# One layer's mixture of experts: residual on GpSimd, one sum over eight on VectorE, early relus all on ScalarE, router scratch in PSUM

## What is computed

```python
x = x + 0.5 * _L0_ffn_ref(_layernorm(x), ...)    # 16 experts 128->256->128, gelu, top 2
x = x + _L0_attn_ref(_layernorm(x), ...)         # linear attention over a sequence, gelu
x = x + 0.5 * _L0_ffn_ref(_layernorm(x), ...)
x = x + 0.5 * _L1_ffn_ref(_layernorm(x), ...)    # 16 experts 128->128, relu, top 2
x = x + _L1_attn_ref(_layernorm(x), ...)         # causal linear attention, 16 heads of 8
x = x + 0.5 * _L1_ffn_ref(_layernorm(x), ...)
```

```python
y = jax.nn.relu(jnp.einsum('nh,edh->ned', flat, expert_w) + expert_b[None, :, :])
sel = jnp.take_along_axis(y, flat_idx[:, :, None], axis=1)
out = jnp.sum(sel * flat_w[:, :, None], axis=1)
```

## Time and profile before

| what | value |
|---|---|
| median of 3 runs | 738.96 us (737.16 to 744.51) |
| the profiled execution | 736.88 us, of which the span of the trace 735.2 us |
| PE busy | 656.1 us (89%) |
| DVE busy | 509.0 us (69%) |
| ACT busy | 403.9 us (55%) |
| POOL busy | 214.4 us (29%) |
| granted TensorE clock, mean | 0.955 |

### The profile page before, as it was taken

The page is one execution under the profiler, slowest core; times in us unless marked ns, Lnnn a source line. Parts: engine busy times, 40 slices in busy tenths (PEclk is TensorE's granted clock), DMA queues, the critical chain, the costliest instruction groups (busy, mean ns, idle before and its releaser), DMA issues.

```text
span 735.2 us, 7595 instructions
## 1 busy us (share of the span) xinstructions
PE 656.1 (89%) x2395; PEld 417.7 (57%) x2395; DVE 509.0 (69%) x1139; ACT 403.9 (55%) x795; POOL 214.4 (29%) x148
## 2 busy tenths in 40 slices
PE   3699998999999999999999998999999869868693
PEld 2456565555555565665666665566666445555472
DVE  5587457647446636658599687869776468688887
ACT  4254464546545544766754695584476325745394
POOL 2120010110002202181320364041037136775367
PEclk9899998999999999999999999999999969989897
DMA  8772522053243134512223232103221000000001
GB/s 244 153 152 63 111 58 58 20 97 58 60 105 66 59 68 79 73 26 46 58 58 70 48 58 58 57 3 91 72 41 27 1 0 0 1 0 16 14 1 29
DMA packets 27027, 42.23 MB, mean 57 GB/s; under 512 B 1689, under 2 KB 8938, under 8 KB 26986
## 3 DMA queue, kind: packets, MB, share of 16 engines
q1 hardware_dynamic: 26986, 41.74, 26.5%
HBM read 40.42 MB, written 1.31 MB: 57 GB/s over the span
## 4 chain that ended last, share of the span: by engine, by line
PE 38%; DVE 25%; issue 19%; POOL 11%; ACT 6%; DMA 0%; SPq 0%; DVEq 0%; POOLq 0%; ACTq 0%
PE py L1103 14%; PE ph L882 4%; PE ph L883 4%; PE ph L884 4%; POOL stage L440 3%; POOL rstd L387 3%; POOL stage L444 3%; DVE xn L659 2%; DVE red L769 2%; DVE hw L841 2%; ACT stage L528 2%; DVE stage L766 1%; DVE stage L736 1%; DVE X L771 1%; PE ps L1057 1%
## 5 line engine op out<-in xcount | busy, mean ns | idle before, releaser
L577 ACT ACTIVATE g<-ph,b1col 128x512 f32<-128x512 f32 x256 | 171.9, 689 | 146.6 <-PE ph L884 111.8
L1103 PE MATMUL py<-hw,w2s 128*128 128x512 f32 x512 | 249.0, 611 | 2.4 <-DVE hw L841 2.4
L841 DVE TENSOR_TENSOR hw<-g,bc 128x1024 f32<-128x1024 f32 x128 | 166.1, 1301 | 94.7 <-ACT g L577 93.2
L387 POOL TENSOR_TENSOR rstd<-vare,mhalf 128x4 f32<-128x4 f32 x24 | 36.6, 1524 | 392.2 <-DVE vare L653 392.2
L1103 PEld LDWEIGHTS py<-hw,w2s 128*128 128x128 f32 x512 | 97.6, 194 | 78.5 <-issue 64.9
L882 PE MATMUL ph<-xbh,w1h 128*128 128x512 f32 x256 | 135.1, 528 | 0.0
L528 ACT ACTIVATE stage<-ps,comb 128x128 f32<-128x128 f32 x288 | 84.1, 514 | 44.4 <-PE ps L1013 28.5
L883 PE MATMUL ph<-xbl,w1h 128*128 128x512 f32 x256 | 103.4, 404 | 0.0
L884 PE MATMUL ph<-xbh,w1l 128*128 128x512 f32 x256 | 103.3, 404 | 0.0
L882 PEld LDWEIGHTS ph<-xbh,w1h 128*128 128x128 f32 x256 | 49.9, 195 | 28.5 <-issue 20.6
L883 PEld LDWEIGHTS ph<-xbl,w1h 128*128 128x128 f32 x256 | 50.1, 196 | 24.0 <-issue 17.0
(11 more groups left out here) (207 smaller groups left out, 959.7 us busy)
## 6 DMA issues: line engine op xcount, KB each, us to landing
bc<-comb_rows SPq DMA_DIRECT2D x31, 1024.0 KB, 8.5
stage<-in_L_ffn_W_dram SPq DMA_DIRECT2D x4, 512.0 KB, 6.9
X<-in_L_attn_x_dram SPq DMA_DIRECT2D x4, 256.0 KB, 3.3
bc<-comb_rows SPq DMA_DIRECT2D x4, 256.0 KB, 5.6
out_dram<-X SPq DMA_DIRECT2D x4, 256.0 KB, 2.3
comb_rows<-combT SPq DMA_DIRECT2D x8, 32.0 KB, 2.1
side<-in_L_attn_wq_dram SPq DMA_DIRECT2D x1, 64.0 KB
side<-in_L_attn_wk_dram SPq DMA_DIRECT2D x1, 64.0 KB
```

Of the source, the lines that this page charges most:

```text
L387: nc.gpsimd.tensor_tensor(rstd[:, 0:n], vare[:, 0:n], mhalf[:, 0:n], ALU.pow).then_inc(light["rstd"], 1)
L577: nc.scalar.activation(g[:, s % 2, h, 0:w], ph[:, (HC * s + h) % RING_PH, 0:w], ACT.Gelu, bias=b1col[:, HC * e + h:HC * e + h + 1]).then_i ...
L841: V.tensor_tensor(hw[:, s % RING_HW, :, 0:w], g[:, s % 2, :, 0:w], bc[:, s // GQ % 2, s % GQ, 0:w].unsqueeze(1).to_broadcast([P, HC, w]), ...
L1103: ins = T.matmul(py[:, 0:cols], w2s[:, w], hw[:, s2 % RING_HW, h, 0:cols], start=e2 == 0 and h == 0, stop=False)
```

## The change

- `ACT_GROUPS` becomes (4, 3): for early tiles ACT makes all four groups (16 instructions a tile), and DVE's L756 goes; late tiles stay at 3 and 1.
- POOL adds the two halves of an early tile in one instruction over 1024 numbers. For late tiles it keeps two of 512. The third addition (L444, L766) goes for all tiles.
- DVE sums over eight in one instruction over 1024 numbers, into one of two buffers.
- The residual goes from DVE to POOL, an addition of 128 numbers a tile, one step behind in POOL's program. The factor 0.5 goes into `comb`. ACT's wait for a free buffer is now for the sum (`sum`), not for the residual; `red` is still the residual.
- In the router `lgs`, `oh1`, `selm`, `topf`, `s_all` and `s_rec` lie in the unused half of the PSUM bank `pl`. A light stage after `rt` waits for `comb` in place of `shift`.
- `LIGHT` starts with the chunks 0, 1, 2 in place of 0, 2, 1, and ATT0's second norm comes one place later. `TURNS` is written anew.

```diff
-    ACT_GROUPS = 3
+    ACT_GROUPS = (4, 3)
+    QUARTERED = {(MOE1_A, 0): False, (MOE1_B, 0): False, (MOE1_A, 1): False, (MOE1_B, 1): False}
...
+        small = pl[:, CH // 2:CH]
+        lgs, oh1, selm = (small[:, i * TPC * E:(i + 1) * TPC * E].rearrange("p (t e) -> p t e", t=TPC) for i in range(3))
...
             def f1_(l, c):
...
+                def residual(j):
+                    pool.wait_ge(signal["sum"], n + j + 1)
+                    nc.gpsimd.tensor_tensor(X[:, tile_(c, j)], X[:, tile_(c, j)], total[:, (n + j) % 2, :], ALU.add).then_inc(signal["red"], 1)
...
-                    pool.wait_ge(signal["relu_a"], (n + j + 1) * ACT_GROUPS)
-                    nc.gpsimd.tensor_tensor(r0, r0, r1, ALU.add).then_inc(signal["half"], 1)
+                    if acts == GROUPS:
+                        pool.wait_ge(signal["relu_a"], (n + j + 1) * acts)
+                        both, other = (r[:, j % 2, a * E * D // 2:(a + 1) * E * D // 2] for a in range(2))
+                        nc.gpsimd.tensor_tensor(both, both, other, ALU.add).then_inc(signal["half"], 2)
...
                     yield
+                    if j:
+                        residual(j - 1)
+                        yield
+                residual(ntiles(c) - 1)
+                yield
...
-                                act.wait_ge(signal["red"], n + j - 1)
+                                act.wait_ge(signal["sum"], n + j - 1)
...
-                V.tensor_tensor(comb[:, tiles(c), :], t_(pm), r_(s_rec).unsqueeze(2).to_broadcast([P, n, E]), ALU.mult).then_inc(light["comb"], 1)
+                V.scalar_tensor_tensor(comb[:, tiles(c), :], t_(pm), 1.0 if moe0(l) else 0.5, r_(s_rec).unsqueeze(2).to_broadcast([P, n, E]),
+                                       ALU.mult, ALU.mult).then_inc(light["comb"], 1)
...
-                        r0, r2 = (r[:, j % 2, a * E * D // 4:(a + 1) * E * D // 4] for a in (0, 2))
-                        (klink if late else hlink)(V.tensor_tensor(r0, r0, r2, ALU.add))
-                    if j:
-                        dve.wait_ge(signal["red"], n + j)
-                    (klink if late else hlink)(V.tensor_reduce(sum_[:, :], r[:, j % 2, 0:E * D // 4].rearrange("p (d e) -> p d e", d=D), AX, ALU.add))
-                    xs_ = X[:, tile_(c, j)]
-                    ins = V.scalar_tensor_tensor(xs_, sum_[:, :], 0.5, xs_, ALU.mult, ALU.add)
-                    ins.then_inc(signal["red"], 1)
+                        V.tensor_reduce(sums, r[:, j % 2, 0:E * D // 2].rearrange("p (a d e) -> p d a e", a=2, d=D), mybir.AxisListType.XY, ALU.add).then_inc(signal["sum"], 1)
...
-                    signal = {"ln": "xl", "rt": "shift", "ct": "ct"}[last]
+                    signal = {"ln": "xl", "rt": "comb", "ct": "ct"}[last]
```

More of the change, by code:

```diff
@@ L114, in build_program @@
         topi = sb("topi", [P, TPC, 8], mybir.dt.uint32)
[L115 to L118, removed]
+        shf, exs = (sb(n, [P, TPC, E]) for n in ("shf", "exs"))
+        oh2, pm = (sb(n, [P, TPC, E]) for n in ("oh2", "pm"))
+        s_top, s_den = (sb(n, [P, TPC]) for n in ("s_top", "s_den"))
         comb = sb("comb", [P, TILES, E])
@@ L156, in build_program @@
         ps = ctx.enter_context(nc.psum_tensor("ps", [P, 3, CH], f32))
+        small = pl[:, CH // 2:CH]
+        lgs, oh1, selm = (small[:, i * TPC * E:(i + 1) * TPC * E].rearrange("p (t e) -> p t e", t=TPC) for i in range(3))
+        topf = small[:, 3 * TPC * E:3 * TPC * E + 2 * TPC].rearrange("p (t a) -> p t a", t=TPC)
+        s_all, s_rec = (small[:, 3 * TPC * E + i * TPC:3 * TPC * E + (i + 1) * TPC] for i in (2, 3))
         def by_tile(buffer, i):
@@ L203, in build_program @@
                                           "vz", "o_ps", "o", "x")}
-        f1 = {(l, late): {n: sem(f"f{l}_{late}_{n}") for n in ("y_ps", "relu_a", "relu_v", "half", "quarter", "red")}
+        f1 = {(l, late): {n: sem(f"f{l}_{late}_{n}") for n in ("y_ps", "relu_a", "relu_v", "half", "quarter", "sum", "red")}
               for l in (MOE1_A, MOE1_B) for late in (0, 1)}
@@ L434, in f1_ @@
                 r = rel_late if late else rel
+                acts = ACT_GROUPS[late]
+                total = red_late if late else red
+                def residual(j):
+                    pool.wait_ge(signal["sum"], n + j + 1)
+                    nc.gpsimd.tensor_tensor(X[:, tile_(c, j)], X[:, tile_(c, j)], total[:, (n + j) % 2, :], ALU.add).then_inc(signal["red"], 1)
                 for j in range(ntiles(c)):
-                    pool.wait_ge(signal["relu_a"], (n + j + 1) * ACT_GROUPS)
@@ L442, in f1_ @@
-                    if l == MOE1_A:
+                    if acts == GROUPS:
+                        pool.wait_ge(signal["relu_a"], (n + j + 1) * acts)
+                        both, other = (r[:, j % 2, a * E * D // 2:(a + 1) * E * D // 2] for a in range(2))
+                        nc.gpsimd.tensor_tensor(both, both, other, ALU.add).then_inc(signal["half"], 2)
+                    else:
+                        pool.wait_ge(signal["relu_a"], (n + j + 1) * acts)
+                        nc.gpsimd.tensor_tensor(r0, r0, r2, ALU.add).then_inc(signal["half"], 1)
+                        pool.wait_ge(signal["relu_v"], (n + j + 1) * (GROUPS - acts))
+                        nc.gpsimd.tensor_tensor(r1.rearrange("p (d e) -> p d e", d=D), r1.rearrange("p (d e) -> p d e", d=D),
+                                                r3.rearrange("p (e d) -> p d e", d=D), ALU.add).then_inc(signal["half"], 1)
@@ L443, in f1_ @@
+                    if QUARTERED[l, late]:
                         pool.wait_ge(signal["half"], 2 * (n + j + 1))
-                        nc.gpsimd.tensor_tensor(r0, r0, r2, ALU.add).then_inc(signal["quarter"], 1)
+                        nc.gpsimd.tensor_tensor(r0, r0, r1, ALU.add).then_inc(signal["quarter"], 1)
                     yield
+                    if j:
[3 more added lines that the diff above has]
+                yield
@@ L520, in f1_ @@
                     for q in range(GROUPS):
-                        if q < ACT_GROUPS:
+                        if q < acts:
                             u = (n + j) * GROUPS + q
@@ L747, in f1_ @@
                 late, signal, n = moe1(l, c)
-                banks, r, sum_ = (ph, rel_late, red_late) if late else (ps, rel, red)
+                banks, r, total = (ph, rel_late, red_late) if late else (ps, rel, red)
+                acts = ACT_GROUPS[late]
                 for j in range(ntiles(c)):
                     for q in range(GROUPS):
-                        if q >= ACT_GROUPS:
+                        if q >= acts:
                             if j == 0:
@@ L760, in f1_ @@
                         yield
-                    if l == MOE1_A:
+                    if n + j >= 2:
+                        dve.wait_ge(signal["red"], n + j - 1)
+                    sums = total[:, (n + j) % 2, :]
+                    if QUARTERED[l, late]:
                         dve.wait_ge(signal["quarter"], n + j + 1)
+                        V.tensor_reduce(sums, r[:, j % 2, 0:E * D // 4].rearrange("p (d e) -> p d e", d=D), AX, ALU.add).then_inc(signal["sum"], 1)
                     else:
                         dve.wait_ge(signal["half"], 2 * (n + j + 1))
-                        r0, r2 = (r[:, j % 2, a * E * D // 4:(a + 1) * E * D // 4] for a in (0, 2))
-                        (klink if late else hlink)(V.tensor_tensor(r0, r0, r2, ALU.add))
-                    if j:
-                        dve.wait_ge(signal["red"], n + j)
-                    (klink if late else hlink)(V.tensor_reduce(sum_[:, :], r[:, j % 2, 0:E * D // 4].rearrange("p (d e) -> p d e", d=D), AX, ALU.add))
-                    xs_ = X[:, tile_(c, j)]
-                    ins = V.scalar_tensor_tensor(xs_, sum_[:, :], 0.5, xs_, ALU.mult, ALU.add)
-                    ins.then_inc(signal["red"], 1)
+                        V.tensor_reduce(sums, r[:, j % 2, 0:E * D // 2].rearrange("p (a d e) -> p d a e", a=2, d=D), mybir.AxisListType.XY, ALU.add).then_inc(signal["sum"], 1)
                     yield
```

19 lines of the change are left out of this document (8 added, 11 removed), and 37 rows, old and new, of the table TURNS.

## The result

The changed kernel takes 715.52 us (median of 4 runs, 707.71 to 716.92), the kernel before 741.49 us in the same session (4 runs). The ratio is 0.963, with a 95% interval of 0.954 to 0.972: 20 to 34 us faster. I had forecast 730.5 with a range from 721 to 744, so the sign was right and the time lies outside the range. The profiled execution took 716.92 us, its span is 714.9 us: 20.3 less than before. The medians lie 26.0 us apart. The profile of before is of an execution faster than any of its four timed ones, that of after is of the slowest of four, so the profiles say where 20.3 us went and nothing of the rest. Ratios are of fast runs only; an execution 1.5% or more above the fastest of its kernel counts as slow, and as e5's profile is of such a one, no marks are read from it.

What follows compares the result with a forecast made beforehand. PE was taken to bound the main stream, a chain across engines the tail. Main part +1.5 and tail -10.0 gave -8.5 us, from the median 738.96 to 730.5, with a range of 721 to 744.

Steps and rivals of the forecast that it cites:

- That part is bound by PE: Main stream, 40 to 575 us: PE busy 513 of 535 us, so PE bounds it; main part forecast at +1.5 us.
- ACT's relus in the main part: Main part: 13.4 us of relus added on ACT, mostly hidden; +2.5 us in all, ends -1 and +13.
- rival 2: MOE1 stretches of the main stream: ACT's relu bursts delay gelus and PE stands; slower, 747.4 us, chance 0.13.
- The router: Sixteen router passes with six results in PSUM, and the wait for `comb` in place of `shift`: 0 us.
- 642 to 650 us: Tail, ATT1's last norm: ACT with its 64 relus takes the place of DVE, 0 us.
- 655.9 to 662.8 us: Tail: the epilogue on POOL and DVE ends before attention needs POOL, PE's wait goes; -4.5 us, ends 1.7 and 6.8.
- 668 to 691 us: Tail chain: two sums of 1.22 replace additions, sums, residual and relu near 5.1 us; -2.6 us, ends 0 and 5.
- the last norm and router: Tail, 691 to 706 us: addition, sum and residual ahead of `xn` go, router pairs lighter; -2.0 us, ends 0 and 2.6.
- Behind the last `comb`: End of the kernel, after 705.8 us: ACT's 76 relus set the pace, 25.7 for 26.6 us; -0.9, ends 0 and 2.
- The tail: From 575 to 735 us, a chain going from engine to engine; its four terms were to save 10.0 us.
- Rival 1: Norms or residuals wait for POOL and the gain is taken back: 738.4 us; chance 0.27, including two-input additions remaining on DVE.
- Rival 3: The lock between DVE and POOL cost more than counted: 16.4 us gained in the tail, 722.6 us, chance 0.15.

Runs made afterwards that it cites:

- e5: The changed kernel, but DVE folds the two halves with an addition of two SBUF inputs and sums over four; 714.84 us, ratio 0.963.
- e1: The changed kernel's instructions in the order of the kernel before (its LIGHT and TURNS); 735.2 us, ratio 0.993 to the kernel before.
- e2: The changed kernel's order with the old epilogue and the router in SBUF, early relus still all on ACT; 728.28 us, ratio 0.982.
- e7: Changed instructions in the old order, but early tiles' fourth relu back on DVE and POOL's early halves as two additions; 727.19 us, ratio 0.982.
- e3: The changed kernel with the router's six results back in SBUF, nothing else changed; 715.68 us, ratio 0.965.
- e4: The changed kernel with the residual on DVE as an addition of two SBUF inputs, none on POOL; 713.74 us, ratio 0.964.
- e13: The kernel before with 17 of PE's norm transposes two main half steps later; 756.24 us, ratio 1.017.
- e14: The changed kernel with 16 of PE's norm transposes one main half step later and the residual on DVE; 718.69 us, ratio 0.965.

## Why the prediction was wrong, point by point

- **"That part is bound by PE, and a faster DVE alone buys nothing there."** The second half stands: e1, with a faster DVE, ends the main stream 1.5 us earlier. The first half is the step that failed. 513 of 535 us busy left 22 us of idle PE, I had the new table before me, and I priced what it changes in the main part at nothing: +1.5 in place of -12.8. What the runs showed in its place is that the order alone takes PE's idle time in the main stream from 21.2 us to 11.7 with the old epilogue (e2), and to 9.4 with the new one. The view of PE's waits would have shown 9.1 us for `xn`, and the two tables that most of PE's norm steps move later. I had used that motion only to call the router's wait harmless.
- **ACT's relus in the main part, +2.5.** PE waited 1.7 us for a gelu, once. Near enough; rival 2 fell. That in the old order these relus, together with POOL's long addition, cost about 8 us (e1 against e7), 5 of them in the tail, I had not seen.
- **The router, 0.** Right for the whole time (e3) and for the wait: no transposes of a norm wait for `comb` in the view of waits. In the tail it isn't nothing, as e3's cast shows. There I had a guess of 0.8 for pairs of SBUF inputs, where the largest item is a cast with one; I had compared where instructions read when they run alone, and what shows here is where the cast writes while POOL is at work.
- **642 to 650 us, 0.** Right in kind: ACT took DVE's place, with the 64 relus, which took 16.73 us where I had 17.9. From attention's result to this `xbh` 1.2 us were gained.
- **655.9 to 662.8 us, -4.5.** The piece went and PE's wait for `X` with it, but from attention's result to the next `comb` (629.5 to 666.9 before) only 1.8 us were gained. What is late next is PE itself, as I had said in kind: in the chain that ended last it works from 634.6 to 646.4 us without a pause, on attention's products and the tiles'. ACT's 40 relus at 654.3 hold the stretch behind it. The chain after:

```profile
633.19 0.57 ACT xbh L496
...
634.62 0.55 PE ph L1049
...
644.38 1.34 PE ph L1061 x12
...
646.55 0.31 DVE pl L701
```

- **668 to 691 us, -2.6; the last norm and router, -2.0.** Between the marks 1.8 and 1.7. Near, and nearer with the sums put right: the terms that I listed for the first come to 4.5 us and not 5.1, which leaves 2.0; in the second, half of what the addition loses in company is 0.5 and not 0.8, so that 1.7 is left there. Of the router the cast alone, 0.84 us before and 0.17 after, gives 0.7.
- **Behind the last `comb`, -0.9.** 28.7 for 29.2 us of span, so 0.5 in place of 0.9. Counted as I had, to the end of the last residual, it is 26.2 for 26.6.
- **The tail.** -7.5 for my -10.0, of which 1.4 and 0.3 lie where I had counted nothing. As a whole it was the better part of the forecast, in part by luck, since the largest term (4.5) brought no more than 1.8. Rival 1 (gain taken back) fell, though one of its signs came: beside POOL's L450 one norm of the tail took 3.43 us for 1.11. It ended while ACT was still at its 64 relus, so no cost of it shows there. Rival 3's 722.6 came nearest, but its 16.4 us were to come from the tail, with 0 in the main part.

The last 30 us went as described: ACT closed up, the others behind it. Timeline of ACT, POOL and DVE after, as in the earlier trace rows:

```profile
692.67 7.49 ACT L549 ACTIVATE stage<-ps,comb 128x128 f32<-128x128 f32 x28
...
703.96 3.57 ACT L549 ACTIVATE bc<-ph,comb 128x128 f32<-128x128 f32 x12 [0.70 <-PE ph L1034]
...
707.61 1.26 POOL L453 TENSOR_TENSOR bc<-bc 128x512 f32<-128x512 f32 x1 [0.23 <-ACT bc L549]
708.82 1.52 POOL L455 TENSOR_TENSOR bc<-bc 128x512 f32<-128x512 f32 x1
...
710.44 1.22 DVE L792 TENSOR_REDUCE red_late<-bc 128x128 f32<-128x1024 f32 x1 [2.39 <-POOL bc L455]
...
711.74 0.45 POOL L443 TENSOR_TENSOR X<-X,red_late 128x128 f32<-128x128 f32 x1 [0.99 <-DVE red_late L792]
```

The durations that I had bounded from other rows came out close. From the groups of the page after (count, busy us, mean ns):

```profile
L450 POOL TENSOR_TENSOR stage<-stage 128x1024 f32<-128x1024 f32 x24 | 57.3, 2387 | 69.8 <-ACT stage L549 69.8
...
L792 DVE TENSOR_REDUCE red<-stage 128x128 f32<-128x1024 f32 x24 | 29.2, 1216 | 21.5 <-POOL stage L450 21.1
```

POOL's addition over 1024 took 2.39 (I took 2.3), DVE's sum 1.22 (1.22), POOL's residual 0.46 at the median (0.6).

No kernel of the study beats the changed one. e4, with the residual left on DVE, measures the same (ratio 0.964 for 0.963).

## What to carry to other kernels

A stretch in which one engine is 96% busy is not settled by that: list what that engine waited for, and if an order is written anew, ask of each such item whether the new order moves it, by how much, and what stands behind it in the queue. Short waits of an engine that carries a stream add up, and the place that avoids them can be one step wide: in the new table one half slot earlier cost 10 us of the main stream; in the old one a half slot later gained 4 to 11 us in all, and two lost 1.7%. Before two profiles are compared mark by mark, look at the clock of each stretch. And when single parts of a change measure nothing, undo them in pairs before calling them worthless, and look at the stretch in which they act.

## What the runs showed that I had not expected

- DVE's sum over 1024 is not held up by POOL at all. All 32 took between 1.21 and 1.22 us, those beside POOL's additions too, where the two-input residual of 128 numbers in e4 ran from 0.29 to 2.47 us. This agrees with the Trainium skill, page "SBUF — State Buffer", section "Who interferes with whom", which says that a reduction never contends with GpSimd on this chip and that an addition of two SBUF inputs does. The views of these lines (instructions; shortest, median and longest ns). After:

```profile
L792 DVE TENSOR_REDUCE red<-stage x24: 1205/1220/1222, 313.8 to 703.1; 128x128 f32<-128x1024 f32 x24
```

e4:

```profile
L795 DVE TENSOR_TENSOR X<-X,red x24: 291/292/2466, 317.0 to 700.4; 128x128 f32<-128x128 f32 x24
```

- DVE's cast of 128x8, which reads and writes SBUF, took up to 1.86 us beside POOL's addition (e3) and 0.17 in every router when it wrote to PSUM.
- ACT's relus of 128 numbers in a row of 64 run at 0.26 us each, where rows of 24 had shown 0.28.
- PE's granted clock was 0.95 from 93 to 572 us in e13, which idled 31.0 us there, and 0.98 before, with 18.8 us idle. Whether the waits brought it down the runs don't settle: e14 was at 0.95 too, with 12.1 us idle.
